# The dense stage's first normalisation and weight splits move into the first attention

## The reference

```python
# attention: 16 heads of 8 channels, buckets of 64 tokens, each sees itself (causal) and the bucket before
h   = layernorm(x) * ln1_g + ln1_b
qkv = h @ w_qkv + b_qkv
...
x   = x + softmax(mask(q k^T * scale)) v @ w_out + b_out          # called x1 in the kernel
h2  = layernorm(x) * ln2_g + ln2_b
x   = x + gelu(h2 @ w1 + b1) @ w2 + b2                            # 128 -> 512 -> 128
# then post-layernorm, and a dense mixture: 8 experts 128 -> 512 -> 128 on every token,
# weighted by gate logits of which only those over a threshold (the k-th smallest of all) count
out = sum_e gate_e * (gelu(x @ w1_e + b1_e) @ w2_e + b2_e)
```

## Time and profile before

| | us |
|---|---|
| median of three runs | 1062.89 (1061.83 to 1063.31) |
| profiled execution: its span, the only time that the page gives of it | 1062.5 |
| first attention | 0 to about 244 |
| dense stage | about 244.5 to about 690 |
| second attention and routed experts | the rest |

### The profile page before, as it was taken

How to read it: one execution, slowest core, us unless ns; L and a number is a source line. 1 busy time by engine, 2 the same in 40 slices (tenths; PEclk the granted TensorE clock), 3 DMA queues, 4 the chain that set the end, 5 groups by cost and what they waited for, 6 DMA issues and landing times. The chain is left out here.

```text
span 1062.5 us, 28952 instructions
## 1 busy us (share of the span) xinstructions
PE 944.1 (89%) x10222; PEld 607.5 (57%) x10222; DVE 859.6 (81%) x2328; ACT 756.3 (71%) x1476; POOL 405.7 (38%) x568
## 2 busy tenths in 40 slices
PE   5999999994889999999999999678888874899996
PEld 3788888872445444444444444246666653788862
DVE  4988988845888999868899999848888866888854
ACT  2666666645889888888888878346767653688854
POOL 3544444443354100000000000023478867676653
PEclk9999999967899999999999999969999985999998
DMA  8333333000002200032212222010111102232318
GB/s 268 123 107 107 107 106 108 24 3 20 1 6 74 72 1 1 1 104 70 77 71 75 87 66 74 20 53 22 32 52 51 54 27 74 75 86 82 85 45 221
DMA packets 61005, 72.60 MB, mean 68 GB/s; under 512 B 8875, under 2 KB 37805, under 8 KB 60865
## 3 DMA queue, kind: packets, MB, share of 16 engines
q1 hardware_dynamic: 50080, 59.36, 17.9%
q0 software_dynamic: 4544, 8.60, 2.4%
q10 hardware_dynamic: 6240, 2.79, 1.1%
HBM read 40.14 MB, written 31.49 MB: 67 GB/s over the span
## 5 line engine op out<-in xcount | busy, mean ns | idle before, releaser
L808 ACT ACTIVATE d__hf<-d__HB,dense__d 128x512 f32<-128x512 f32 x288 | 184.7, 679 | 39.2 <-PE d__HB L1047 38.2
L867 DVE TENSOR_TENSOR d__hl<-d__hf,d__hh 128x1024 f16<-128x1024 f32 x144 | 173.6, 1219 | 20.4 <-ACT d__hh L813 18.1
L813 ACT ACTIVATE d__hh<-d__hf 128x1024 f16<-128x1024 f32 x144 | 152.2, 1057 | 4.6
L781 POOL TENSOR_SCALAR d__rstd<-d__mv 128x4 f32<-128x4 f32 x16 | 14.2, 886 | 353.6 <-DVE d__mv L990 353.6
L1045 PE MATMUL d__YB<-d__hh,d__w2h 128*128 128x512 f16 x288 | 110.5, 384 | 2.5 <-DVE d__tmp L924 2.5
L1046 PE MATMUL d__HB<-d__xl,d__w1h 128*128 128x512 f16 x288 | 110.9, 385 | 0.0
L1045 PE MATMUL d__HB<-d__xh,d__w1h 128*128 128x512 f16 x288 | 110.8, 385 | 0.0
L1047 PE MATMUL d__HB<-d__xh,d__w1l 128*128 128x512 f16 x288 | 110.6, 384 | 0.0
L316 POOL TENSOR_SCALAR_AFFINE_SELECT a__pt<-a__pt 128x512 f32<-128x512 f32 x128 | 81.3, 657 | 75.4 <-ACT a__pt L364 75.3
L1046 PE MATMUL d__YB<-d__hl,d__w2h 128*128 128x512 f16 x288 | 110.1, 382 | 0.0
L1047 PE MATMUL d__YB<-d__hh,d__w2l 128*128 128x512 f16 x288 | 109.9, 382 | 0.0
(11 more groups left out here) (402 smaller groups left out, 2544.4 us busy)
## 6 DMA issues: line engine op xcount, KB each, us to landing
rows<-a__blank SPq DMA_DIRECT2D x72, 268.0 KB, 3.2
d__G<-gates SPq DMA_DIRECT2D x64, 256.0 KB, 3.2
c__xin<-rows SPq DMA_DIRECT2D x39, 134.0 KB, 2.2
dense__stage<-e_w SPq DMA_DIRECT2D x16, 256.0 KB, 3.1
b__stage<-e_w SPq DMA_DIRECT2D x32, 128.0 KB, 2.2
c__yb<-parts SPq DMA_DIRECT2D x8, 256.0 KB, 8.4
c__yb<-parts ACTq DMA_DIRECT2D x8, 256.0 KB, 8.9
out<-c__xo SPq DMA_DIRECT2D x8, 256.0 KB, 2.3
```

The costliest lines, as they stand in the source:

```text
L808: act.activation(hf[:, q, f], HB[:, f], gelu, scale=1.0 / WS, bias=b1[:, at:at + 1]).then_inc(s_["h_free"], 1)
L813: act.activation(hh[:, j % (LEAD + 1), f - 1:f + 1], hf[:, q, f - 1:f + 1], ACT.Copy).then_inc(s_["hi_done"], 1)
L867: dve.tensor_tensor(hl[:, p, f], hf[:, q, f], hh[:, p, f], ALU.subtract).then_inc(s_["lo%d_done" % i], 1)
```

## The change

- **In the first attention.** Each step gets new entries. "norm1" (ScalarE, end of part 3): the attention's own normalisation, as an activation with the inverse root as scale and -mean x inverse root as bias; the bias ("shift2") is made by two GpSimd instructions under "norm". "stats" and the power now do up to four tiles: two of x and, from step 5 on, two of x1 (the block that was finished in that step). "norm2" (ScalarE, part 3): the second normalisation, for the first 14 of the 16 blocks. It is transposed by TensorE in the next step's "output". "halves2" (part 1): ScalarE evicts it as h2 and writes its high half, GpSimd the low half. "split" (ScalarE, end of part 3, steps 2 to 19): scales half a set of weights in place and writes its high half. "wlow" (GpSimd, end of part 0, steps 3 to 20): its low half. SP's fetches of weight sets 2 to 8 stand among the blank transfers. The gelu's table is loaded by ScalarE at its list's end.
- **In the dense stage.** Steps begin at -2. Statistics, normalisation, lift and halves are left for the last chunk alone and are done once, behind `hidden(0)` on TensorE and ScalarE and ahead of everything on VectorE and GpSimd. The weight splits and their fetches are gone. Both subtractions to the low half stay together up to step 8.
- xh, xl and the split weights are allocated outside of both stages.

```diff
@@ PARTS_0
-     ("copy", 4, 1)],
+     ("copy", 4, 1), ("wlow", 0, 0)],
...
-     ("weights", 3, 1), ("values", 3, 0)],
+     ("weights", 3, 1), ("values", 3, 0), ("halves2", 6, 0)],
...
-     ("weights", 3, 3), ("values", 3, 2)]]
+     ("weights", 3, 3), ("values", 3, 2), ("norm1", 0, 0), ("norm2", 5, 0), ("split", 0, 0)]]
+AHEAD = NB - 2
+CUTS = 2 * (E + 1)
@@ parts_0
+                elif what in ("stats", "norm"):
+                    if s < AHEAD + 5:
+                        step(what, s, k)
+                elif what in ("halves2", "norm2"):
+                    if 0 <= s - stage < AHEAD:
+                        step(what, s - stage, k)
+                elif what == "split":
+                    if 0 <= s - 2 < CUTS:
+                        step(what, s - 2, k)
+                elif what == "wlow":
+                    if 0 <= s - 3 < CUTS:
+                        step(what, s - 3, k)
@@ attention_0
+        def both_norms(n):
+            return slice(0 if n < NB else 2, 4 if n >= 5 else 2)
@@ sync
+                if i % 10 == 0 and i >= 20:
+                    sp.wait_ge(w_low, i // 5 - 2)
+                    keep["fetch_set"](sp, i // 10)
                 if i % 5 == 0:
                     sp.wait_ge(hn_done, i // 5 + 1)
...
+            sp.wait_ge(w_low, 2 * E - 2)
+            keep["fetch_set"](sp, E)
@@ gpsimd
+                wait(pool, norm2_done, n - 5)
+                wait(pool, hn_done, min(n, NB))
...
-                t.link(pool.tensor_scalar(rstd[:], mv[:, :, 1], EPS, 1.0, ALU.add, ALU.mult))
-                pool.tensor_tensor(rstd[:], rstd[:], half[:], ALU.pow).then_inc(rstd_done, 1)
+                t.link(pool.tensor_scalar(rstd[:, v], mv[:, v, 1], EPS, 1.0, ALU.add, ALU.mult))
+                pool.tensor_tensor(rstd[:, v], rstd[:, v], half[:, v], ALU.pow).then_inc(rstd_done, 1)
...
+                if what == "norm" and n:
+                    v = both_norms(n)
+                    pool.wait_ge(rstd_done, n + 1)
+                    pool.tensor_scalar(shift2[:, v], mv[:, v, 0], -1.0, 1.0, ALU.mult, ALU.mult).then_inc(shift2_own, 1)
+                    pool.wait_ge(shift2_own, n)
+                    pool.tensor_tensor(shift2[:, v], shift2[:, v], rstd[:, v], ALU.mult).then_inc(shift2_done, 1)
+                if what == "halves2":
+                    pool.wait_ge(xh_done, n + 1)
+                    pool.tensor_tensor(xl[:, toks2(n)], h2[:], xh[:, toks2(n)], ALU.subtract).then_inc(xl_done, 1)
+                if what == "wlow":
+                    pool.wait_ge(w_high, n + 1)
+                    pool.tensor_tensor(cut_of(("w1l", "w2l"), n), stage[:, n // 2 % 2, n % 2],
+                                       cut_of(("w1h", "w2h"), n), ALU.subtract).then_inc(w_low, 1)
@@ scalar
+                if what == "norm2":
+                    act.wait_ge(shift2_done, n + 5)
+                    wait(act, out_full, n + 1 if n else 0)
+                    for a in range(2):
+                        ins = act.activation(hn2[:, a, :], keep["x1"][:, 2 * n + a, :], ACT.Identity,
+                                             scale=rstd[:, 2 + a:3 + a], bias=shift2[:, 2 + a:3 + a])
+                    ins.then_inc(norm2_done, 1)
+                if what == "norm1" and n:
+                    act.wait_ge(shift2_done, n)
+                    wait(act, lift_full, n)
+                    for a in range(2):
+                        ins = act.activation(hn[:, a, :], x[:, 2 * n + a, :], ACT.Identity, scale=rstd[:, a:a + 1],
+                                             bias=shift2[:, a:a + 1])
+                    ins.then_inc(hn_done, 1)
+                if what == "halves2":
...
+                    act.wait_ge(x1_own, n + 2)
+                    wait(act, xl_done, n)
+                    act.activation(h2[:], WB[:, TB:2 * TB], ACT.Identity, scale=cols2[:, 0:1],
+                                   bias=cols2[:, 1:2]).then_inc(h2_done, 1)
+                    act.wait_ge(h2_done, n + 1)
+                    act.activation(xh[:, toks2(n)], h2[:], ACT.Copy).then_inc(xh_done, 1)
+                if what == "split":
+                    j, a = n // 2, n % 2
+                    act.wait_ge(keep["wl%d" % (j % 2)], 32 * (j // 2 + 1))
+                    v = stage[:, j % 2, a]
+                    act.activation(v, v, ACT.Copy, scale=WS).then_inc(scaled, 1)
+                    act.wait_ge(scaled, n + 1)
+                    act.activation(cut_of(("w1h", "w2h"), n), v, ACT.Copy).then_inc(w_high, 1)
             parts_0(step)
+            act.wait_ge(warm, 1)
+            act.activation(scrap[:], half[:, 0:2], ACT.Gelu).then_inc(warm, 1)
@@ vector
                 if what == "stats":
...
+                    lns = range(4)[both_norms(n)]
...
+                    for a in lns:
+                        v = x[:, 2 * n + a, :] if a < 2 else keep["x1"][:, 2 * (n - 5) + a - 2, :]
+                        sums.inc(dve.bn_stats(st[:, a, :], v))
...
-                if what == "norm":
+                if what == "norm" and n == 0:
@@ tensor
                 if what == "output":
...
+                    if 0 < n <= AHEAD:
+                        pe.wait_ge(norm2_done, n)
+                        wait(pe, h2_done, n - 1)
+                        for a in range(2):
+                            pe.transpose(WB[:, TB + a * P:TB + (a + 1) * P], hn2[:, a, :], ident[:])
@@ dense_0
-BEGIN, END = -LEAD - 3, JOBS + 3
+BEGIN, END = -LEAD, JOBS + 3
+LAST = M_JOBS - 1
...
             def whole_low(s):
-                return M_JOBS <= s + LEAD + 3 and s - 1 < M_JOBS
+                return s - 1 < M_JOBS
@@ dense_0, tensor
             def hidden(j):
...
-                pe.wait_ge(s_["xl0_done" if kind == "m" else "xl1_done"], c + 1)
-                pe.wait_ge(s_["w_done"], 1 if kind == "m" else e + 2)
+                if j == LAST:
+                    pe.wait_ge(s_["xl0_done"], 1)
+                if kind == "e":
+                    pe.wait_ge(s_["xl1_done"], c + 1)
...
-                c = s + LEAD + 2
-                if 0 <= c < M_JOBS:
-                    wait(pe, s_["qb_free"], right[("lift", c)])
-                    pe.wait_ge(s_["hn_done"], c + 1)
+                if s == BEGIN:
+                    pe.wait_ge(s_["hn_done"], 1)
                     turned(QB, "qb_full", lambda a: hn[:, a, :])
```

More of the change, by code:

```diff
@@ L190, in attention_0 @@
         x = m.sb("x", [P, NT, C])
[L191 to L194, removed]
+        st = m.sb("st", [P, 4, 6])
+        mv = m.sb("mv", [P, 4, 2])
+        half = m.sb("half", [P, 4])
+        rstd = m.sb("rstd", [P, 4])
+        shift2 = m.sb("shift2", [P, 4])
+        hn2 = m.sb("hn2", [P, 2, C])
+        h2 = m.sb("h2", [P, TB])
         hn = m.sb("hn", [P, 2, C])
@@ L388, in step @@
                 if what == "stats":
-                    rows_landed(dve, n)
                     wait(dve, rstd_done, n)
[L392 to L395, removed]
-                    settle(dve, passed_dve)
[L397 to L402, removed]
+                    wait(dve, shift2_done, n - 1)
+                    lns = range(4)[both_norms(n)]
+                    if n < NB:
+                        rows_landed(dve, n)
+                    for a in lns:
+                        v = x[:, 2 * n + a, :] if a < 2 else keep["x1"][:, 2 * (n - 5) + a - 2, :]
+                        sums.inc(dve.bn_stats(st[:, a, :], v))
+                    sums.wait()
+                    settle(dve, passed_dve)
+                    for a in lns:
+                        ins = dve.bn_aggr(mv[:, a, :], st[:, a, :])
+                        ins.then_inc(var_done, 1) if a == lns[-1] else sums.inc(ins)
+                if what == "norm" and n == 0:
+                    dve.wait_ge(rstd_done, 1)
                     dve.tensor_scalar(hn[:, 0, :], x[:, 2 * n, :], mv[:, 0, 0:1], rstd[:, 0:1],
@@ L644, in uses_0 @@
             left.append(("logits", s - 2))
-        if 0 <= s + LEAD + 2 < M_JOBS:
-            right.append(("lift", s + LEAD + 2))
+        if s == BEGIN:
+            right.append(("lift", LAST))
         if 0 <= s - COUNT_0 <= ROUNDS + 1:
@@ L750, in _ @@
         def _(sp):
[L751 to L755, removed]
             keep["fetch_att"](sp)
@@ L996, in _ @@
                     fold(s + 2)
-                c = s + LEAD + 3
-                if 0 <= c < M_JOBS:
-                    for a in range(4):
-                        first.inc(dve.bn_stats(st0[:, a, :], x1[:, 4 * c + a, :]))
-                    first.wait()
-                    settle(dve, s_["passed_dve"])
-                    for a in range(4):
-                        ins = dve.bn_aggr(mv0[:, a, :], st0[:, a, :])
-                        ins.then_inc(s_["var0_done"], 1) if a == 3 else first.inc(ins)
                 if whole_low(s):
@@ L2225, in fetch_dense, with fetch_set @@
                 sp.dma_start(d32[:], d["d32"]).then_inc(keep["d32_in"], 16)
[L2226 to L2230 removed]
+                for j in range(2):
+                    fetch_set(sp, j)
```

(8 more changed lines are left out.)

108 lines of the change are left out of this document (47 added, 61 removed).

## The result

The changed kernel took **1073.59 us** (median of four runs, 1071.82 to 1074.37), the kernel before 1063.1 in the runs beside it: a ratio of 1.0087, 95% interval 1.0063 to 1.0112. It is 0.9% slower, where a faster kernel of 1056 had been forecast, and the time lies outside the range of 1045 to 1070. The profiled execution (1071.82 us, the shortest of the four) has a span of 1070.1 us, against 1062.5 before. Its 7.6 us come from three places. The start of the first attention's last eviction (aT) is 33.0 us later (275.17 against 242.13, forecast 22). The dense stage gives back 29.3, counted from there to the first gelu of job 15, as forecast (29). Another 3.8 come behind it.

What follows compares the result with a forecast made beforehand. TensorE and VectorE's chain to the low half of q and k were taken as level in the attention. Attention 12.5 + 6.6 + 3 = 22 slower, dense stage 29 faster, from 1062.5: 1056 us, range 1045 to 1070.

Steps and rivals of the forecast that it cites:

- The dense stage: After the attention: first product some 10.2 us earlier and shorter steps (7.2 us), 29 us gained, bounds 23 and 31.
- The weight's low half: First attention, GpSimd behind group 0's causal pair: holds VectorE's cast or subtraction, 0.87 us a step, 1.05 in two early steps; 12.5 in all.
- the end of its range (1.6): First attention: 1.6 us a step if the x1 sum's second addition also collides with the next causal pair.
- The sign that was given: First attention: group 0's cast lasting near 0.8 to 1 us, ending with the weight's low half on GpSimd.
- The normalisations' going from VectorE: First attention: VectorE's two normalisations lie just ahead of its wait for TensorE's scores, so removing them gains nothing.
- The power: First attention, GpSimd ahead of group 2's causal pair: delays TensorE 0.6 us a step, 11 steps, 6.6; ends 0 and 0.83.
- The clock: Granted clock in the first attention: one earlier fall was seen, nothing charged for it in the sum, kept as a rival.
- rival 2: First attention: the clock falls at TensorE's waits of 0.9 and 0.6 us, 1.7 a step, 20 more: 1076; chance 0.20.
- The tail: First attention, steps 17 to 20: ScalarE's new work stands ahead of needed evictions, 3 us in all (1 to 5).
- The sum: Whole kernel: attention 22 us slower, dense stage 29 faster, 1062.5 to 1055.5; predicted 1056 us.
- steps 3 and 4: Early first attention: the weight's low half costs 1.05 us in each, 2.1 together.
- What was said to show it wrong: Attention step under 14.2 or over 15.8, clock below 1.00 between 50 and 215 us, or dense steps over 8.

Runs made afterwards that it cites:

- Experiment 1: Changed kernel with GpSimd's weight low half moved from behind the causal pair of group 0 to the end of part 1: 1045.9 us, ratio 0.9835 to the kernel before.
- experiment 4: Changed kernel with the attention's own normalisation (norm1) put back from ScalarE on VectorE, all else as in the change: 1054.4 us, ratio 0.9918 to the kernel before.
- experiment 7: Changed kernel with weight low half at part 1's end, power behind group 2's causal pair, and norm1 back on VectorE: 1032.75 us, ratio 0.9711.
- experiment 2: Changed kernel with GpSimd's power moved behind the causal pair of group 2 instead of ahead of it: 1068.41 us, ratio 1.0045 to the kernel before.
- experiment 6: Changed kernel with ten unread identity transposes put into TensorE's wait for the low half of q and k: 1064.41 us, ratio 1.0001 to the kernel before.

## Why the prediction was wrong, point by point

**The dense stage: right.** The first product comes with the stage's first instruction (277.75 and 277.80), job 5's first gelu 29.8 us behind it (forecast 30), job 11's 73.5 (forecast 73, before 102.3), a step takes 7.29 (forecast 7.2). The gain was 29.3, and 29.0 to 29.2 in each of the six experiments that kept the whole dense part.

**The weight's low half: the step that failed.** The place and the kind of collision were right; the term of 0.87 us a step was too small. Experiment 1 prices the insertion at 1.38 us a step. The 0.87 allowed for a cast that slips in and a subtraction that is held, with a ScalarE that is 0.35 us late. ScalarE was 0.55 late, which adds 0.2, and the second addition met the next causal pair, which adds 0.5: together the 1.57 us by which the low half is late, of which the 0.18 of the cast stay in experiment 1, so that 1.39 should go there. The prediction had named that second collision as the end of its range (1.6), and it came in 11 of 12 full steps. Whether it would have been spared at 0.35 us no run shows. The sign that was given, a cast of 0.8 to 1 us, belongs to a ScalarE that is on time, as in experiment 4: with both moves the step falls there from 14.92 to 13.21 (experiment 7), and if 0.80 of these 1.71 are the power's, as in experiment 2, 0.9 are left for the weight's low half. The normalisations' going from VectorE was said to gain nothing: they cost nothing that shows when they are put back, but on ScalarE they cost 0.79 us a step.

**The power: right place, a little small.** 0.6 forecast, 0.80 measured (experiment 2), within its bounds of 0 and 0.83.

**The clock: a term put at nothing.** It was kept out of the sum, as rival 2. It fell behind 5 of the 11 waits of 1.64 us: in four of the steps between the evictions, at 0.7 to 2.2 us per fall (1.7 in rival 2), and in step 16. The falls hang on the term that was too small: with the wait that the forecast had, 0.86 us in experiment 4, the clock doesn't fall in these steps. So rival 2's 1076 lies near the measured time by luck. It had a fall in each of 12 steps, behind waits no longer than the forecast's. The Trainium skill's rule that the prediction cited ("TensorE: Matmul & The Clock Gate", Part 1, "A second HAM failure mode") has the clock swing when TensorE idles briefly between groups of products; the rows agree for some of the waits of 1.6 us, and not for those of 0.9 and 0.6 us in experiment 4.

**The tail: right in size.** From the eviction of step 16 to the last one, 3.9 us were forecast (3 and one step's 0.87) and 4.1 measured. With the waits filled (experiment 6) it is 2.0.

**The sum.** Up to the eviction of step 5 the forecast had 2.1 us (steps 3 and 4); measured is -0.4. These two steps cost 0.4 each, and an early one is shorter by 1.4, which it is in some of the experiments and not in others. The 11 steps from there to step 16 were forecast at 16.2 (11 x 1.47) and took 29.3 more: 25.0 without the falls (11 x 2.27) and 4.3 for the falls. With the tail's 4.1 (3.9) that makes 33.0 against 22. With the dense stage's 29.3 the span would be 1066.3. The other 3.8 us of the profiled span lie outside the change: 3.0 of them at the start of the second attention (713 to 725 us), where the granted clock rises some 9 us later, counted from that stage's start, than in the profile before. The same place gives +3.0 in experiment 6 and -3.0 in experiment 7, and at most 0.5 in the others, so it comes and goes with the execution; what decides it was not tried.

**What was said to show it wrong** did: steps over 15.8 us, and a clock below 1.00 between 50 and 215 us.

## What to carry to other kernels

An instruction put on GpSimd held every short VectorE instruction between SBUF tiles (a cast, a subtraction, an addition) that came while it ran, so it isn't free because GpSimd is idle; look for the stretch in which VectorE reads PSUM or waits, and move the insertion there (here by one entry of a list, for 28 us). Where a collision is priced from a timeline, move the rows against each other by the uncertainty of their starts, and follow the whole chain behind the first one that is held: here a ScalarE that is 0.55 us late instead of on time brought 0.79 us a step (experiment 4). And a wait on TensorE can cost more than its length, when the products behind it run at the lower clock.

## What the runs showed of the hardware that had not been expected

- A single wait of 1.64 us in a stretch that is otherwise full of products could let the granted clock fall to 0.50, from 0.1 us before the wait's end to 0.8 us behind it, for 3.4 to 6.8 us. It did so behind 5 of 11 such waits in the changed kernel's profile, and behind 7 of 11 in the second experiment's, where the same wait stands in a shorter step. Waits of 0.9 and 0.6 us in one step did not (experiment 4), but a wait of 0.95 in step 17 of the same run, which has no projections, was followed by a fall at 238.8. What decides stays open.
- Work that does nothing made the kernel faster: 1.1 us of transposes in each wait, 9.2 us off the total.
- Two short VectorE instructions in a row can be held by two GpSimd instructions in a row: the cast, held by the causal pair (which ended at 153.64), ended at 153.69, and the subtraction, which reads what the cast writes and starts at 153.73, had to wait for all of the next GpSimd instruction, whose row starts at 153.60.
